# W1 as plain fp32 in TensorE's array, brought per tile by a transfer of SyncE

## The reference

```python
x = x + 0.5 * ffn(layernorm(x))
x = x + attention(layernorm(x))
x = x + 0.5 * ffn(layernorm(x))

def ffn(tgt):                    # E = 8 experts, D = 128, F = 512
    logits = tgt @ Wr.T + br
    top_v, top_i = top_k(logits, 2)
    router_w = one_hot(top_i) weighted with softmax(top_v)
    h = relu(einsum('bsd,efd->bsef', tgt, W1) + b1)
    o = einsum('bsef,edf->bsed', h, W2) + b2
    return layer_norm(tgt + einsum('bsed,bse->bsd', o, router_w)) * gamma + beta
```

## Time and profile before

| | |
|---|---|
| median of 3 runs | 822.25 us (819.69 to 822.4) |
| profiled execution, its own time | 824.45 us |
| its span, first to last instruction | 822.6 us |
| mean granted TensorE clock | 0.891 of full speed |
| TensorE busy | 636.6 us, 77% of the span |
| VectorE busy | 540.3 us, 66% |
| ScalarE busy | 416.9 us, 51% |
| GpSimd busy | 384.9 us, 47% |

### The profile page before, as it was taken

The page is one execution under the profiler, slowest core; times in us unless marked ns, Lnnn a source line. Parts: engine busy times, 40 slices in busy tenths (PEclk is TensorE's granted clock), DMA queues, the critical chain, the costliest instruction groups (busy, mean ns, idle before and its releaser), DMA issues.

```text
span 822.6 us, 16274 instructions
## 1 busy us (share of the span) xinstructions
PE 636.6 (77%) x3708; PEld 522.6 (64%) x3708; DVE 540.3 (66%) x1790; ACT 416.9 (51%) x955; POOL 384.9 (47%) x415
## 2 busy tenths in 40 slices
PE   2554699998999679885897778787899949889910
PEld 2453599997878556663665455654788839778800
DVE  4555677666787588795699475852668625477626
ACT  3643255554446367565647644663554514546621
POOL 5454044454354047258257312503646754566543
PEclk9955699999999989997998799897999978999965
DMA  8311244223332001001000001001222411411141
GB/s 288 101 58 58 53 108 98 70 66 102 91 82 56 11 0 39 14 4 37 13 27 20 7 10 43 26 1 46 50 56 67 106 47 37 145 52 55 42 155 51
DMA packets 53675, 49.18 MB, mean 60 GB/s; under 512 B 9862, under 2 KB 45874, under 8 KB 53072
## 3 DMA queue, kind: packets, MB, share of 16 engines
q1 hardware_dynamic: 44736, 31.25, 14.1%
q0 software_dynamic: 8640, 16.87, 6.6%
q10 hardware_dynamic: 208, 0.02, 0.0%
HBM read 25.99 MB, written 23.02 MB: 60 GB/s over the span
## 4 chain that ended last, share of the span: by engine, by line
PE 54%; DVE 16%; issue 10%; POOL 9%; ACT 7%; DMA 3%; DVEq 0%; ACTq 0%; SPq 0%; POOLq 0%
PE banks L859 15%; PE banks L849 8%; PE banks L773 7%; PE banks L774 5%; PE banks L775 5%; PE banks L923 5%; PE banks L817 3%; PE banks L831 2%; POOL zb L422 2%; ACT rowbuf L550 2%; PE banks L808 2%; DVE nb L1378 2%; POOL rows L411 1%; POOL rs L395 1%; DVE sum_r L1245 1%
## 5 line engine op out<-in xcount | busy, mean ns | idle before, releaser
L1209 DVE TENSOR_SCALAR scratch<-banks,biases 128x128 f32<-128x128 f32 x468 | 135.9, 345 | 83.0 <-PE banks L849 75.2
L859 PE MATMUL banks<-w2T,scratch 128*128 x1248 | 167.7, 278 | 2.2 <-DVE scratch L1218 2.2
L859 PEld LDWEIGHTS banks<-w2T,scratch 128*128 128x128 f32 x1248 | 154.1, 195 | 3.2 <-issue 3.1
L594 ACT ACTIVATE scratch<-banks 128x512 f32<-128x512 f32 x156 | 93.0, 596 | 81.8 <-PE banks L775 81.8
L411 POOL DMA_INDIRECT rows<-rowbuf,slot x96 | 95.2, 992 | 68.6 <-issue 36.6
L433 POOL DMA_INDIRECT results<-scratch x78 | 78.0, 1000 | 78.7 <-DVE scratch L1218 62.7
L656 ACT ACTIVATE scratch<-banks,nb 128x1024 f32<-128x1024 f32 x64 | 71.1, 1113 | 81.1 <-DVE nb L1378 80.7
L1378 DVE TENSOR_REDUCE nb<-banks 128x1 f32<-128x1024 f32 x64 | 76.8, 1217 | 48.2 <-PE banks L775 47.0
L849 PE MATMUL banks<-ident,scratch 128*128 128x128 f32 x624 | 95.8, 277 | 0.0
L587 ACT ACTIVATE xnTh<-banks 128x128 fp32r<-128x128 f32 x156 | 43.1, 277 | 101.9 <-PE banks L831 101.8
L849 PEld LDWEIGHTS banks<-ident,scratch 128*128 128x128 f32 x624 | 80.0, 144 | 22.0 <-issue 1.6
(11 more groups left out here) (183 smaller groups left out, 1122.5 us busy)
## 6 DMA issues: line engine op xcount, KB each, us to landing
scratch<-rows SPq DMA_DIRECT2D x156, 64.5 KB
yrows<-scratch SPq DMA_DIRECT2D x78, 64.0 KB, 1.9
scratch<-results SPq DMA_DIRECT2D x3, 1024.0 KB, 6.7
rows<-padrows SPq DMA_DIRECT2D x34, 64.5 KB
x<-in_L_attn_x_dram SPq DMA_DIRECT2D x4, 512.0 KB, 5.7
scratch<-in_L_ffn_W_dram SPq DMA_DIRECT2D x1, 2048.0 KB, 19.3
out_dram<-x SPq DMA_DIRECT2D x4, 512.0 KB, 5.9
rows<-rowbuf,slot POOLq DMA_INDIRECT x96
```

The costliest lines, as they stand in the source:

```text
L594: act.activation(hs[:, k * F:(k + 1) * F], bank(2 + k), ACT.Copy).then_inc(h_sb, 1)
L859: ins = pe.matmul(bank(6, 0, D), hT[:, k * F + c * P:k * F + (c + 1) * P], w2T[:, c * D:][:, bass.ds(at, D)], start=(c == 0), stop=(c == F ...
L1209: ins = dve.tensor_scalar(hT[:, k * F + c * P:k * F + (c + 1) * P], hT_at(k, c), biases[:, c:][:, bass.ds(at, 1)], 0.0, ALU.add, ALU.max)
```

## The change

W1 is no longer kept as two fp32r halves. A buffer `blocks` holds for each expert one block with W1, W2, b1 and b2 in fp32. SP gets a new function `stage`: it reads the slot's offset into a register, waits until TensorE has used the tile of three slots ago, and copies W1 of the slot's expert (128 partitions x 512 values, 256 KB) from `blocks` to one of three fixed places, `w1s`. It does so six slots behind `load`. TensorE's `first` takes the quarters of W1 from there as the stationary operand and the turned x as the moving one, so that h comes out turned, and `turn_h`, the copy of h, the split of x and one ReLU place fall away. `second` of a tile comes in the step of its slot, one step earlier than before, and its result alternates between two banks of PSUM. ScalarE does two ReLUs and VectorE two.

```diff
+    STAGES = 3
-        w1h, w1l = sb("w1h", E * F, F32R), sb("w1l", E * F, F32R)
-        w2T = sb("w2T", E * FC * D)
-        biases = sb("biases", E * BIAS)
+        blocks = sb("blocks", E * BLOCK)
-        Y_BEHIND = 12
+        Y_BEHIND, STAGE_BEHIND = 12, 6
...
+            def stage(p, s):
+                T = SLOTS * p + s
+                at = sp.value_load(block_at[0:1, s:s + 1], min_val=0, max_val=(E - 1) * BLOCK)
+                if T >= STAGES:
+                    wait_apart(sp, (hT_ps, 2 * (T - STAGES) + 2))
+                sp.dma_start(staged(T), blocks[:, bass.ds(at, F)]).then_inc(w1_staged[T % STAGES], 16)
...
             for s in range(SLOTS):
                 if s == 4:
                     pads(0, 1)
                 if s == GSLOTS:
                     group_ready(0, 1)
                 load(0, s)
+                if s >= STAGE_BEHIND:
+                    stage(0, s - STAGE_BEHIND)
                 if s >= Y_BEHIND:
                     write_y(s - Y_BEHIND)
-            for s in range(SLOTS - Y_BEHIND, SLOTS):
-                write_y(s)
+            for s in range(SLOTS, SLOTS + Y_BEHIND):
+                if s < SLOTS + STAGE_BEHIND:
+                    stage(0, s - STAGE_BEHIND)
+                write_y(s - Y_BEHIND)
...
                 if s == GSLOTS:
+                    for t in range(s - STAGE_BEHIND, s):
+                        stage(1, t)
                     group_ready(1, 1)
                 load(1, s)
+                if s >= STAGE_BEHIND and not GSLOTS <= s < GSLOTS + STAGE_BEHIND:
+                    stage(1, s - STAGE_BEHIND)
...
+            for s in range(SLOTS - STAGE_BEHIND, SLOTS):
+                stage(1, s)
...
-            def h_copy(T):
-                act.activation(hs[:, k * F:(k + 1) * F], bank(2 + k), ACT.Copy).then_inc(h_sb, 1)
-            def relu_last(p, s):
+            def copy_xT(T):
+                act.activation(xT_of(T), bank(0, 0, P), ACT.Copy).then_inc(xT_sb, 1)
+            def relu_first(T, at):
+                for c in range(FC // 2):
+                    ins = act.activation(hT_of(T, c), hT_at(T, c), ACT.Relu, bias=blocks[:, B1_AT + c:][:, bass.ds(at, 1)], scale=1.0)
...
-                three(bank(2 + k), xh[:, k * P:(k + 1) * P], xl[:, k * P:(k + 1) * P],
-                      w1h[:, bass.ds(at, F)], w1l[:, bass.ds(at, F)]).then_inc(h_ps, 1)
-            def turn_h(T):
...
+            def first(T):
+                pe.wait_ge(xT_sb, T + 1)
+                pe.wait_ge(w1_staged[T % STAGES], 16 * (T // STAGES + 1))
+                for c in range(FC):
+                    ins = pe.matmul(hT_at(T, c), staged(T)[:, c * P:(c + 1) * P], xT_of(T), start=True, stop=True)
+                    if (c + 1) % (FC // 2) == 0:
+                        ins.then_inc(hT_ps, 1)
...
                 if 0 <= s + 1 < SLOTS:
-                    first(t + 1, w_at[s + 1])
-                if 0 <= s < SLOTS:
-                    turn_h(t)
-                if s >= 1:
-                    second(t - 1, w_at.pop(s - 1))
+                    first(t + 1)
+                if s >= 0:
+                    second(t, w_at.pop(s))
...
-            def x_rest(T):
-            def relu(T, at):
+            def relu_rest(T, at):
+                for c in range(FC // 2, FC):
...
             def step(p, s):
                 t = SLOTS * p + s
+                if s >= 1:
+                    add_b2(t - 1, e_at.pop(s - 1))
+                if 0 <= s + 1 < SLOTS:
+                    relu_rest(t + 1, e_at[s + 1])
```

More of the change, by code:

```diff
@@ L49, in macaron_kernel @@
     QG = 4
-    assert D == P and S == TB * P and F % P == 0 and SLOTS % 2 == 0 and TB % QG == 0
+    assert D == P and S == TB * P and F % P == 0 and SLOTS % 2 == 0 and FC % 2 == 0 and TB % QG == 0
     rows = [nc.dram_tensor(f"rows{g}", [E * REGION + P, ROW], F32).ap() for g in range(2)]
@@ L183, in macaron_kernel @@
         found_rows = sem("found_rows")
-        h_rest = sem("h_rest")
+        hT_first = sem("hT_first")
+        w1_staged = [sem(f"w1_staged{k}") for k in range(STAGES)]
         x_loaded = [sem(f"x_loaded{b}") for b in range(BATCHES)]
@@ L202, in rows_bank, with xT_of, staged, hT_at @@
             return 6 if a < BATCHES else 7
-        def hT_at(k, c):
-            return bank(1, k * P, (k + 1) * P) if c == FC - 1 else bank(4 + k, c * P, (c + 1) * P)
+        def xT_of(T):
+            return xT[:, T % 2 * P:(T % 2 + 1) * P]
+        def staged(T):
+            return w1s[:, T % STAGES * F:(T % STAGES + 1) * F]
+        def hT_at(T, c):
+            return bank(2 + 2 * (T % 2) + 2 * c // FC, c % (FC // 2) * P, (c % (FC // 2) + 1) * P)
+        def hT_of(T, c):
+            return hT[:, (T % 2 * FC + c) * P:(T % 2 * FC + c + 1) * P]
+        def y_at(T):
+            return bank((6, 1)[T % 2], 0, D)
         def o_bank(b, g):
@@ L234, in over_tiles, with expert_offset @@
             return t[:, :].unsqueeze(2).broadcast_to([P, E, TB])
-        def expert_offset(eng, table, step, s):
+        def expert_offset(eng, s):
             _, values = nc.values_load_multi_w_load_instructions(
-                table[0:1, s:s + 1], engines=[eng], min_val=0, max_val=(E - 1) * step,
+                block_at[0:1, s:s + 1], engines=[eng], min_val=0, max_val=(E - 1) * BLOCK,
                 skip_runtime_bounds_check_because="VectorE clamps the table to the last expert")
@@ L327, in _ @@
             group_ready(0, 0)
+            sp.wait_ge(w1_sb, E)
             sp.wait_ge(wT_ps, 2 * E)
@@ L541, in weights @@
                     act.wait_ge(wT_ps, 2 * g + 1)
-                    act.activation(w1h[:, g * F:(g + 1) * F], bank(g % 2), ACT.Copy).then_inc(w_half, 1)
-                    act.wait_ge(wT_ps, 2 * g + 2)
-                    act.activation(w2T[:, g * F:(g + 1) * F], bank(2 + g % 2), ACT.Copy).then_inc(w2_sb, 1)
+                    act.activation(blocks_v[:, g, 0:F], bank(g % 2), ACT.Copy).then_inc(w1_sb, 1)
             def normalise(dst, src, n, tiles=range(TB)):
@@ L829, in turn_x, with second @@
                 if T:
-                    pe.wait_ge(xl_ready, T)
+                    pe.wait_ge(xT_sb, T)
                 pe.transpose(bank(0, 0, P), xt_v[:, r, 0:D], ident[:, :]).then_inc(xT_ps, 1)
-            def first(T, at):
-                k = T % 2
-                pe.wait_ge(xl_ready, T + 1)
-                if T >= 2:
-                    pe.wait_ge(h_sb, T - 1)
-                three(bank(2 + k), xh[:, k * P:(k + 1) * P], xl[:, k * P:(k + 1) * P],
-                      w1h[:, bass.ds(at, F)], w1l[:, bass.ds(at, F)]).then_inc(h_ps, 1)
-            def turn_h(T):
[L842 to L847, removed]
-                for c in range(FC):
[L849 to L860, removed]
+            def first(T):
[5 more added lines that the diff above has]
+                        ins.then_inc(hT_ps, 1)
+            def second(T, at):
+                pe.wait_ge(hT_first, T + 1)
+                pe.wait_ge(hT_sb, T + 1)
+                if T >= 2:
+                    pe.wait_ge(y_sb, T - 1)
+                for c in range(FC):
+                    ins = pe.matmul(y_at(T), hT_of(T, c), blocks[:, W2_AT + c * D:][:, bass.ds(at, D)], start=(c == 0), stop=(c == FC - 1))
                 ins.then_inc(y_ps, 1)
@@ L999, in _ @@
             pe.wait_ge(table_ready, 2)
-            for s in range(-2, SLOTS + 1):
+            for s in range(-2, SLOTS):
                 step(0, s)
@@ L1175, in table @@
                 dve.tensor_scalar(row_of[:, mine], roff[:, :], float(E * REGION), None, ALU.min)
[L1176 to L1177 removed]
+                steps.then(dve.tensor_scalar(block_at[:, mine], eidf[:, :], float(E - 1), float(BLOCK), ALU.min, ALU.mult))
                 dve.tensor_copy(carry[:, :], base[:, :]).then_inc(table_ready, 1)
@@ L1195, in find @@
                 yield
-            def x_rest(T):
[L1198 to L1201, removed]
-            def relu(T, at):
-                k = T % 2
-                dve.wait_ge(hT_ps, T + 1)
+            def relu_rest(T, at):
+                dve.wait_ge(hT_ps, 2 * T + 2)
                 if T >= 2:
                     dve.wait_ge(y_ps, T - 1)
-                for c in range(FC - 1):
-                    ins = dve.tensor_scalar(hT[:, k * F + c * P:k * F + (c + 1) * P], hT_at(k, c),
-                                            biases[:, c:][:, bass.ds(at, 1)], 0.0, ALU.add, ALU.max)
+                for c in range(FC // 2, FC):
+                    ins = dve.tensor_scalar(hT_of(T, c), hT_at(T, c), blocks[:, B1_AT + c:][:, bass.ds(at, 1)], 0.0, ALU.add, ALU.max)
                 ins.then_inc(hT_sb, 1)
             def add_b2(T, at):
-                k, r = T % 2, T % RING
+                r = T % RING
                 dve.wait_ge(y_ps, T + 1)
```

68 lines of the change are left out of this document (26 added, 42 removed).

## The result

| | forecast | measured |
|---|---|---|
| time | 1391 us (1275 to 1470) | 1456.11 us median of 4 runs (1453.36 to 1458.45) |
| against the kernel before, on the same chip | 1.69 | 822.33 us (819.69 to 823.92, 4 runs), ratio 1.771, 95% interval 1.765 to 1.777 |
| profiled execution | 1393 us | 1453.36 us, span 1451.6 |

What follows compares the result with a forecast made beforehand. TensorE was taken to set the pace in pass 0, something else in pass 1. Profiled 824.45 + 40.6 (pass 0) + 516 (pass 1 loop) + 12 (allowance) = 1393, less 2.2 to the median: 1391 us, range 1275 to 1470.

Steps and rivals of the forecast that it cites:

- The closed loop, one tile long: Pass 1: each stage waits behind a load that waits for a send; 10.83 us a tile, +516 us.
- The rival in which the sends land in time: Pass 1 has no loop, only SP's queue at 2.36 us a slot; 865 us in all, chance 0.03.
- The slow transfer: Landing of the W1 copy takes 4.9 us, adding 151 us over 62 turns; 1542 us, chance 0.05.
- Faster: TensorE's gain shows in pass 0 and the unpaced part of pass 1: 41 us less, 781 us, chance 0.01.
- the 0.50 that the forecast named as a sign: Pass 1: TensorE stands 7 us a tile for the stage, with granted clock 0.50; 1.00 would show the forecast wrong.
- The price of 1.71 a turn: Pass 1 loop: half clock instead of full costs 1.71 us a turn, 106 us over 62 turns.
- SP's own pace, pass 0: Stage adds 1.12 us to SP's load and write, 2.76 us a slot; with one stall, pass 0 takes +40.6 us.
- The stall at slot 39: Pass 0: load 39 waits for slot 31's scatter, with stage 33 behind it; 7.4 us added.
- The turn: One round of the pass 1 loop, landing through first, second, send and load to the next stage: 10.83 us.
- The allowance of 12: Pass 1: +12 us for VectorE's routing and merging pieces and two 1024 KB reads meeting the turn.
- TensorE's gain: Where TensorE is the bound, W1 as fp32 saves 0.34 us a tile, 1.81 us against 2.15.
- the full-clock loop: Rival: pass 1 loop runs at full clock, 9.12 us a turn, 106 us less; 1285 us, chance 0.10.

Runs made afterwards that it cites:

- the two runs that lengthen the loop: Changed kernel with the stage 5 or 3 slots behind the load instead of 6: 1101.46 us (one run) and 926.77 us (ratio 1.128 to the kernel before).
- the one that takes SP out of it: Changed kernel with the W1 transfers issued by ScalarE, three tiles ahead, instead of SP: 788.76 us, ratio 0.961 to the kernel before.

## Why the prediction was right, and where it was short

**The mechanism.** The closed loop, one tile long, was the forecast's main term, and it is what happened: stages about 11 us apart, each 1.1 us behind a load, that load 2.4 us behind a send, TensorE standing 7.1 us for each (7.10 in the turn above). That this was the cause and not a companion is shown by the two runs that lengthen the loop and by the one that takes SP out of it. The rival in which the sends land in time, 865 us, falls with the 64 waits for them. The slow transfer falls with a landing of 704.31 - 701.88 = 2.43 us, forecast 2.46. *Faster* was rightly put down to SP's slot: with SP relieved the kernel is faster, at 788.76 where 781 was worked out for it.

**The clock.** In the loop all 64 groups of `first` took 2.04 to 2.06 us for their eight instructions, the half-clock figure. The granted clock over longer stretches was 0.57 to 0.64 and not the 0.50 that the forecast named as a sign. The turn shown above tells why (columns as in the windows above):

```profile
704.50:707.50 3.00, 3.00 (x15) 3.00 (x16) 0.99 (x9) 0.63 (x2) 0.00 (x0) 0.50 0.00 0
708.50:711.00 2.50, 0.00 (x0) 0.00 (x0) 0.01 (x1) 0.04 (x1) 1.49 (x3) 1.00 0.01 3
712.00:714.00 2.00, 0.00 (x0) 0.00 (x0) 0.00 (x0) 0.00 (x0) 0.83 (x3) 0.50 0.12 35
```

While TensorE works the level is 0.50; as its work ends it rises to 1.00, TensorE then stands, and before the next tile comes it is 0.50 again. The faster level is granted, but to a standing engine; in 14 of 62 turns it came early enough to shorten the W2 products (1.55 to 1.86 us for 1.91). The price of 1.71 a turn held against 11.08 - 9.34 = 1.74.

**SP's own pace, pass 0: the step that was mis-sized.** The stage was priced at 1.12 us, the pitch of a load by itself, with an upper bound of 1.24. A slot cost 3.34 and not 2.76, so the stage costs 1.70 within it. The terms from the timeline: load to stage 1.11, as forecast; stage to write 0.61, since the issue of this copy takes 0.50 and not 0.33; the write's issue 0.53 and not 0.36; the TENSOR_LOAD behind it 0.54 and not 0.27. These three excesses, 0.16, 0.17 and 0.27, add up to 0.60. I had looked for the stage's price in the one row nearest in kind and had not asked what it does to its neighbours. Between the load of slot 12 (109.74, forecast 109.6) and the last load (340.87) lie 65 slots: 65 x 0.58 = 38 of the missing 50 us. Another 7 are longer slots, such as 188.84 to 192.61. In eight of them the issue of the write itself took 0.65 to 1.86 us (up to 1.37 before the change); SP's list of waits names nothing for this stretch, and the cause stays open. 3 are the five closing stages at 2.16 for 1.61; 2 are the last tiles. The stall at slot 39 was 8.47 - 1.62 = 6.9 us for 7.4.

**The turn.** 11.2 and 11.1 us for 10.83. In most turns landing 2.42, second 1.91, the ways to VectorE and GpSimd 0.15 and 0.86, and load to stage 1.12 are within 0.04 us of the forecast. `first` is 706.15 - 704.31 = 1.84 and not 1.71: I had taken the figure of a group that followed other products, and a group that begins after a wait is longer, 2.05 us busy for 1.91 at half clock, 1.13 for 1.06 at full. Send to load has a median of 2.48 (2.36 in the turn shown, up to 2.95 in others), for 2.33. Over 62 turns the excess is 20 us: 8 of `first`, 11 of send to load, 7 of VectorE's pieces, which lengthen the two ways in some turns, less 6 for landings and W2 products that were shorter. The allowance of 12 was meant for the pieces, which took 7; that the rest of it stood in for the other two terms is luck.

**TensorE's gain.** A tile came to 1.89 us and not 1.81, measured where nothing else paces: the gain is 0.26 us a tile. `first` took its 0.89 (in the fence above 122.45 - 121.56), but from the turn of x to the next `first` pass 0.11 us there, and the forecast's period left 0.03 for it. It is a gain all the same, and it had no part in the time of the changed kernel, where TensorE waits.

The range held: the lower end was the full-clock loop, and the upper bound of SP's stage (1.24) was too low, since it left out what a copy does to the next two instructions. The time stayed in the range because the turn, the larger term, was nearly right.

One alternative was not tried: reading W1 in place as the stationary operand, which would need no transfer at all; whether the operand's address can come from a register there, no run here shows.

## What to carry to other kernels

Before a DMA is put on a queue that works in order, write down what stands ahead of it there and what that waits for: the new one inherits each of these waits, and if one of them depends on the work that the new one feeds, a loop is closed whose length is a distance in the issue order, not the number of buffers. An engine with idle time and a queue of its own, and with the register already loaded, made of the same change a gain of 4% (0.961) instead of a loss of 77%. When an issue is priced, take a row of its own form, with both sides in SBUF if it has them, and price the instructions behind it as well: here they carried 0.44 of the 0.60 us that were missing in a slot.

## What the runs showed of the hardware

- A copy from SBUF to SBUF takes 0.50 us of its sequencer to issue, on SP as on ScalarE (0.49), where a load of rows takes 0.34. It is the same for 256 and for 64 KB.
- The write issued right behind such a copy takes 0.53 us, for 0.36 to 0.37 before, at either size. In the changed kernel's three slots where it was issued 0.94 us after the start of the copy and not 0.61, it took 0.33 twice (once at 190.89).
- A TENSOR_LOAD on SP behind that copy and the write takes 539 ns in the median at 256 KB and 272 at 64 KB, and 444 when ScalarE issues the 256 KB, with SP's queue free of them. The Trainium skill, "DMA: Bandwidth & Descriptors", section "Latency and other measured facts", has about 600 ns as the least that it takes; the rows go down to 262, and come near to it only with this traffic (up to 686).
- The transfer lands after 2.43 us for 256 KB and after 1.97 for 64 KB: four times the size costs 0.46 us more.
- TensorE's half clock in a loop with 7 us of standing could be lifted by work that nobody reads: 0.59 to 0.99 in the same stretch, worth some 1.4 to 1.7 us in a turn of 11. Without it the granted clock is 1.00 in a part of the stand (708.5 to 711.0) and 0.50 when work comes.
